# A LoRA residual on one core: the order of TensorE's work per group of four sequences

## The reference

```
B_sel = B[adapter_ids]
A_sel = A[adapter_ids]
Bx  = einsum('bni,bri->bnr', x, B_sel)
out = einsum('bnr,bor->bno', Bx, A_sel) * 1.0
return x + out
```

## Time and profile before

| | us |
|---|---|
| median of 3 runs | 92.24 (92.05 to 92.42) |
| the profiled execution | 92.24, with a span of 90.4 |
| TensorE busy | 80.0, 89% of the span |
| VectorE, ScalarE, GpSimd busy | 59.5, 59.1, 60.6 |
| DMA | 34.82 MB, 385 GB/s over the span |
| mean granted TensorE clock | 0.971 of full speed |

### The profile page before, as it was taken

How to read it: one execution, slowest core, us unless ns; L and a number is a source line. 1 busy time by engine, 2 the same in 40 slices (tenths; PEclk the granted TensorE clock), 3 DMA queues, 4 the chain that set the end, 5 groups by cost and what they waited for, 6 DMA issues and landing times.

```text
span 90.4 us, 3605 instructions
## 1 busy us (share of the span) xinstructions
PE 80.0 (89%) x1469; PEld 63.4 (70%) x1469; DVE 59.5 (66%) x106; ACT 59.1 (65%) x153; POOL 60.6 (67%) x136
## 2 busy tenths in 40 slices
PE   3999999999999999899999999999999999942600
PEld 3999997878686878577878786868787878720200
DVE  0039940319596959692949596959696969599950
ACT  2368498986868777659685968677786969450000
POOL 6000849999697969785969696979797978360000
PEclk9999999999999999999999999999999999999855
DMA  3899999999999999999999999999999999977695
GB/s 36 350 410 412 421 413 406 404 412 410 399 410 408 412 410 410 393 413 410 406 406 417 410 424 402 426 413 413 412 422 408 421 397 415 373 303 317 259 404 223
DMA packets 8945, 34.82 MB, mean 385 GB/s; under 512 B 482, under 2 KB 482, under 8 KB 8930
## 3 DMA queue, kind: packets, MB, share of 16 engines
q1 hardware_dynamic: 8784, 34.08, 94.2%
q10 hardware_dynamic: 146, 0.52, 1.5%
HBM read 17.83 MB, written 16.78 MB: 383 GB/s over the span
## 4 chain that ended last, share of the span: by engine, by line
PE 70%; DMA 14%; DVE 6%; SPq 2%; DVEq 1%; issue 1%; ACT 1%
PE t_bank L221 32%; PE y_banks L252 19%; PE bx_bank L232 19%; DMA x_all<-in_x 14%; DVE x_all L365 4%; DVE bx_parts L356 2%; SPq L135 2%; DVEq L49 1%; ACT bx_parts L287 1%; SPq L131 0%
## 5 line engine op out<-in xcount | busy, mean ns | idle before, releaser
L365 DVE TENSOR_TENSOR x_all<-y_banks,x_all 128x1024 f32<-128x1024 f32 x32 | 39.3, 1230 | 15.9 <-PE y_banks L252 15.3
L305 ACT COPY x_t<-t_bank 128x512 f32<-128x512 f32 x64 | 34.5, 592 | 14.5 <-PE t_bank L221 13.9
L171 POOL CAST a_duo<-a_table 128x512 fp32r x64 | 36.8, 619 | 3.5 <-PE y_banks L252 2.2
L221 PE MATMUL t_bank<-ident,x_all 128*128 128x128 f32 x256 | 34.8, 279 | 0.2 <-DMA x_all<-in_x 0.2
L161 POOL COPY b_duo<-b_table 128x256 f32 x64 | 22.9, 403 | 15.8 <-PE bx_bank L232 8.7
L221 PEld LDWEIGHTS t_bank<-ident,x_all 128*128 128x128 f32 x256 | 27.6, 141 | 7.3 <-issue 5.5
L252 PE MATMUL y_banks<-a_duo,bx_parts 64*128 64x512 f32 x128 | 20.1, 421 | 3.7 <-ACT bx_parts L287 3.2
L232 PE MATMUL bx_bank<-x_t,b_duo 128*32 128x64 f32 x1024 | 21.2, 222 | 0.0
L232 PEld LDWEIGHTS bx_bank<-x_t,b_duo 128*32 128x32 f32 x1024 | 16.1, 109 | 5.5 <-issue 5.4
L356 DVE TENSOR_TENSOR bx_parts<-bx_bank,bx_parts 32x64 fp32r<-32x64 f32 x64 | 14.1, 220 | 4.8 <-ACT bx_parts L320 3.7
L252 PEld LDWEIGHTS y_banks<-a_duo,bx_parts 64*128 64x128 f32 x128 | 10.7, 184 | 7.2 <-issue 3.8
(11 more groups left out here) (10 smaller groups left out, 5.4 us busy)
## 6 DMA issues: line engine op xcount, KB each, us to landing
x_all<-in_x SPq DMA_DIRECT2D x6, 2048.0 KB, 22.2
out_y<-x_all SPq DMA_DIRECT2D x3, 2048.0 KB, 20.9
out_y<-x_all SPq DMA_DIRECT2D x6, 1024.0 KB, 10.5
out_y<-x_all SPq DMA_DIRECT2D x8, 512.0 KB, 3.8
x_all<-in_x SPq DMA_DIRECT2D x3, 1024.0 KB, 20.9
x_all<-in_x SPq DMA_DIRECT2D x2, 512.0 KB, 6.2
x_all<-in_B ACTq DMA_DIRECT2D x1, 512.0 KB, 4.8
x_all<-in_A SPq DMA_DIRECT2D x1, 512.0 KB, 4.6
```

Source lines behind the costliest of these rows:

```text
L171: last = nc.gpsimd.tensor_copy(a_duo[duo % 2][:, k, :], a_table[:, bass.ds(adapters[k] * BANK, BANK)])
L221: last = nc.tensor.transpose(t_bank[unit % 2][:, c * P:(c + 1) * P], x_all[:, 2 * duo + tile, at:at + P], ident[:, :])
L305: nc.scalar.copy(x_t[duo % 2][:, half * HALF:(half + 1) * HALF, tile, :], t_bank[unit % 2][:, :].rearrange("p (c n) -> p c n", c=HALF)).th ...
L365: nc.vector.tensor_tensor(here, product, here, ALU.add).then_inc(y_drained, 1)
```

## The change

TensorE's loop runs T0 T1 (d+1), then the whole down product of duo d, then T2 T3 (d+1), then U (d-1). ScalarE's `split_high(d)` stands between the copies of T1 and T2 of duo d+1, and `double_parts(d)` behind the copy of T3. VectorE runs `split_rest(d)` ahead of both adds of duo d-1, except for the last duo, whose `split_rest(15)` stands between the two adds of duo 14. The load of tiles 4 to 7 becomes two loads of two tiles.

```diff
-    LOADS = [(0, 1), (1, 2), (2, 4)] + [(t, t + 4) for t in range(4, 24, 4)] + [(24, 26), (26, 30), (30, 32)]
+    LOADS = [(0, 1), (1, 2), (2, 4), (4, 6), (6, 8)] + [(t, t + 4) for t in range(8, 24, 4)]
+    LOADS += [(24, 26), (26, 30), (30, 32)]
...
-            def down(duo, first, end):
-                if first == 0:
-                    pe.wait_ge(b_gathered, duo + 1)
-                pe.wait_ge(t_copied, B_UNITS + UNITS * duo + (3 if end <= HALF else 4))
-                for c in range(first, end):
+            def down(duo):
+                pe.wait_ge(b_gathered, duo + 1)
+                pe.wait_ge(t_copied, B_UNITS + UNITS * (duo + 1))
+                for c in range(CHUNKS):
...
-                down(duo, 0, HALF)
+                down(duo)
                 if duo + 1 < DUOS:
                     transpose_unit(duo + 1, 2)
                     transpose_unit(duo + 1, 3)
-                down(duo, HALF, CHUNKS)
                 if duo:
                     up(duo - 1)
...
                     copy_x(duo + 1, 0)
                     copy_x(duo + 1, 1)
-                if duo:
-                    double_parts(duo - 1)
+                split_high(duo)
                 if duo + 1 < DUOS:
                     copy_x(duo + 1, 2)
                     copy_x(duo + 1, 3)
-                split_high(duo)
-            double_parts(DUOS - 1)
+                double_parts(duo)
...
             split_rest(0)
-            for duo in range(1, DUOS):
+            for duo in range(1, DUOS - 1):
+                split_rest(duo)
                 add_x(duo - 1, 0)
-                split_rest(duo)
                 add_x(duo - 1, 1)
+            add_x(DUOS - 2, 0)
+            split_rest(DUOS - 1)
+            add_x(DUOS - 2, 1)
             add_x(DUOS - 1, 0)
             add_x(DUOS - 1, 1)
```

More of the change, by code:

```diff
@@ L235, in down @@
                                                 start=(c == 0), stop=(c == CHUNKS - 1))
-                if end == CHUNKS:
-                    last.then_inc(bx_done, 1)
+                last.then_inc(bx_done, 1)
             def up(duo):
```

## The result

The changed kernel takes 95.71 us (median of 6 runs, 95.23 to 96.01) against 92.29 for the kernel before: a ratio of 1.036, with a 95% interval of 1.033 to 1.039. It is slower; 90.0 was forecast. The profiled execution has a span of 94.2.

A forecast was written before the change was run, and what follows sets the result against it. TensorE's chain bounds the loop, with DMA close behind. Loop 1.7 us less and tail 0.9 less put the compute chain's span at 87.9; stores set 88.2, so 90.0 us against 92.24, own range 89.6 to 90.6.

The forecast's parts named there:

- some 1.3 us are small hiccups, which I keep: TensorE's loop, duo 3 to duo 15: 53.3 us against 52.0 for 12 periods of 4.33; the excess was kept unchanged.
- TensorE without a break: Reading of the kernel before: from 15.95 us on the chain that ended last is TensorE alone, 4.33 us per duo.
- The period: TensorE's time per duo in the loop: 1.02 + 1.03 + 1.02 + 1.13 = 4.20 us instead of 4.33, bounds 4.05 and 4.56.
- the edge from transposes to up: New edge in TensorE's loop, priced like transposes to down, inside the 1.02; could save 0.15 or cost 0.36 us.
- The drain at a change of tiling mode: TensorE drains between transposes (128 rows) and up (64 rows); pauses of 0.17 and 0.36 us seen, sum stays at 4.20.
- The start: First duos: the wait for the load until 15.91 us gives way to one for ScalarE, T0 of duo 2 at 16.1; no gain.
- The tail: VectorE from add (13, 0) on: six adds and one `split_rest`, 8.4 us against 9.33, so 0.9 less.
- The floor of the stores: After 77.0 us, 4.18 MB left at 413 GB/s take until 87.1; gives a span of 88.15, setting the end.
- The 3.37 us from the last add to the span's end: End of the kernel: last add ends at 87.03, the span 3.37 later with the last store; kept for the new kernel.
- Its 1.3 us from an add to its store's data: Tail stores: a store's data starts about 1.3 us behind its add, so each tile is there in time, the last by 0.1.
- The slower rival: Up behind transposes pays another 0.36 us in each duo: period 4.56, last add 88.8, time 94.0 us; chance 0.06.
- The clock rival: Start: 16 transposes together at half the clock take 1.8 us more; with the loop 1.8 later, 91.8 us; chance 0.02.

The follow-up runs named there:

- e4: Kernel before, with the down products of duos 6 and 15 computed seven times in a row; instruction pieces 6.20 and 5.92 us apart with full DMA engines, 3.73 quiet.
- e8: Kernel before with halves up to duo 13 and the changed kernel's order on all three engines for duo 14 alone; 92.39 us against 92.48, ratio 0.9995.
- e2: Changed kernel with the old loads, one load of four tiles for tiles 4 to 7; 95.63 us against 95.71 for the changed kernel.
- e1: Kernel before with only the down product joined ahead of T2 and T3, loads and other engines' orders kept; 96.45 us, ratio 1.044.
- e3: Kernel before with the down product in quarters, one behind each transposing unit; 99.46 us, ratio 1.074.
- e5: Changed kernel with half of the down product's matmuls left out (chunks 0 to 3 only); 90.59 us in one execution.
- e6: Changed kernel with every store held until all 32 tiles are done; measured time not given, no pauses after the DMA share falls to 0.01 from 50 us on.
- e13: Changed kernel with transfers of one tile and at most five in flight; 95.59 us, ratio 1.033.
- e12: Changed kernel with transfers of one tile and at most four in flight; 97.08 us, ratio 1.041.
- e11: Changed kernel with transfers of one tile and at most three in flight; 104.77 us, ratio 1.127.

## Why the prediction was wrong

- **The step that failed: "some 1.3 us are small hiccups, which I keep".** They were a resource at its limit, and the prediction carried them over as a constant. It read the chain as "TensorE without a break", though the 0.39 us pause at 37.93 stands in it. A piece of 256 instructions needs 5.9 to 6.2 us with full DMA engines (e4), and the order before used one up in 5.7 to 7.0 (starts of every 126th matmul in e8, which has this order up to duo 13); where a fetch had started early, a short piece passed without a pause. The changed kernel's pauses sum to 5.8 us in the chain and more by the matmuls' starts: 57.3 us for 12 periods (78.49 - 21.18) where 12 x 4.20 + 1.3 = 51.7 were forecast, and 0.8 before them.
- **Why this edit woke it.** Not the smaller loads (e2) and not ScalarE's order (e1). A joined down product is 64 matmuls in 1.03 us; a piece with most of two such products lasts 5.0 to 5.4 us, and TensorE waits for the rest. In quarters there is no pause (e3), with half the product left out none (e5), with quiet DMA engines none (e6). This accounts for 3.1 of the 5.1 us of pauses in the loop. The other 2.0 (0.56, 1.23, 0.17) stand behind pieces that TensorE took 6.2 us or more for, where the fetch itself came late; e1, e3 and e5 show that they come with the joined order (the 1.23 was 0.39 before), but what delays those fetches is open.
- **The period, right:** 4.20 us, and the edge from transposes to up costs what the edge to down does. The drain at a change of tiling mode, named from the Trainium skill (TensorEngine Tiling, Key Properties), fits as far as a pause shows: weight loads pause 0.17 us there (timeline of the kernel after, the weight loads of an up product):

```profile
39.08 0.77 PEld L251 LDWEIGHTS y_banks<-a_duo,bx_parts 64*128 64x128 f32 x8 [0.17 <-issue]
```

- **The start, right:** the load is waited for no longer, and T0 of duo 2 starts at 15.94 behind ScalarE (16.1 forecast). The two small loads bring nothing (e2).
- **The tail, right in shape:** one VectorE chain of 8.6 us (8.4 forecast, 9.33 before).
- **The floor of the stores, nearly right:** a span of 88.2 forecast, 88.7 in e5, where nothing else binds, and 90.5 in e8 with the last add at 85.8. At most 1.7 us could be had (92.3 against e5's 90.6), and e8 shows that even 1.2 us of it in the compute chain comes to nothing. The 3.37 us from the last add to the span's end, which the prediction took as fixed, are 3.2 in the changed kernel and 4.6 in e8. Its 1.3 us from an add to its store's data are 1.06 by its own figures (88.09 - 87.03), which moves nothing.
- **The slower rival had the right sign and the wrong mechanism:** a period of 4.56 everywhere (94.0 us), where a period of 4.20 with a pause in most pieces came (95.7). I had given slower 0.06. The row that should have raised it was there: pauses named "issue" in the middle of a product that waits for nothing.
- **The clock rival fell:** the granted clock was 1.00 through the loop (windows from 20 to 77 us).

## What to carry to other kernels

TensorE's instructions are traffic too; no run here looked at another engine's. Where the DMA engines are full, divide TensorE's instructions by 256 and compare the time of each such piece with 6.2 us, a bound that some pieces here overran by 2 us; a reordering that packs short instructions together can cost more than the edges it saves, though the work is the same. A pause marked "issue" in the middle of a product is no noise: count the matmuls between two of them before keeping them as a constant. And when two limits lie within 2 us, look at what the second allows before pricing the first.

## What the runs showed of the hardware

- A 16 KB piece of TensorE's instructions (256) came 5.9 to 6.2 us after the one before with full DMA engines, and 3.7 both at a DMA share of 0.62 and at 0.03 (e4); in real orders some came only after 8.
- Matmuls of 128x32 by 64 columns in four column groups follow each other at 16 ns (64 in 1.03 us, changed kernel).
- The DMA engines were full (408 GB/s) with five transfers of 0.5 MB in flight, and moved 362 GB/s with four and 304 with three (e13, e12, e11, 20 to 44 us).
